# A fused attention and expert kernel on one core: keys folded before the split, token copies on ScalarE, attention copies on VectorE, later sums

## What is computed

```python
latent = (xn @ Wk + xn @ Wv) @ W_down_kv
q, k, v = heads(xn @ Wq), heads(latent @ W_up_k), heads(latent @ W_up_v)   # 16 heads of 8
scores = clip(q @ k.T / sqrt(128)) * exp(-1e-4 * abs(i - j))
attention = softmax(scores) @ v @ Wo
...
logits = xn @ Wr.T + br;  top 2 of 8 experts, softmax weights cw
z = xn + sum_e cw[e] * (gelu(xn @ W1[e].T + b1[e]) @ W2[e].T + b2[e])
experts = layer_norm(z) * ln_w + ln_b
```

## Time and profile before

| | |
|---|---|
| median of 3 runs | 271.72 us (271.06 to 271.76) |
| the profiled execution | 271.68 us, its span 269.4 us |
| PE, DVE, ACT, POOL busy | 84%, 73%, 75%, 68% of the span |
| exponentials (ACT) | 128, 1153 ns each as recorded |
| corrections (DVE) | 128, 562 ns |
| scores, outputs (PE) | 49.6 and 66.9 us busy |
| GELUs (ACT) | 156, 369 ns |
| panel copies (DVE) | 39, 996 ns |

### The profile page before, as it was taken

How to read it: one execution, slowest core, us unless ns; L and a number is a source line. 1 busy time by engine, 2 the same in 40 slices (tenths; PEclk the granted TensorE clock), 3 DMA queues, 4 the chain that set the end, 5 groups by cost and what they waited for, 6 DMA issues and landing times.

```text
span 269.4 us, 5034 instructions
## 1 busy us (share of the span) xinstructions
PE 225.9 (84%) x1673; PEld 122.7 (46%) x1673; DVE 196.0 (73%) x466; ACT 200.8 (75%) x335; POOL 182.2 (68%) x186
## 2 busy tenths in 40 slices
PE   0794557989999999998888888998788999999964
PEld 0572143879989899995122212222112231232313
DVE  2837986788988986874787876686967677667641
ACT  2557526445555565659999999999899999999950
POOL 9176708747787855594999999998899999700000
PEclk9998968999999999999999999999999999999995
DMA  6995601432217237311640169211890000000001
GB/s 202 438 439 202 175 22 39 133 134 79 67 53 179 68 74 188 78 27 49 184 112 23 29 164 217 61 29 33 207 202 2 1 21 20 0 39 2 1 39 45
DMA packets 17900, 27.46 MB, mean 102 GB/s; under 512 B 3008, under 2 KB 14944, under 8 KB 17488
## 3 DMA queue, kind: packets, MB, share of 16 engines
q1 hardware_dynamic: 15264, 22.21, 26.9%
q0 software_dynamic: 2272, 4.66, 7.4%
q10 hardware_dynamic: 336, 0.25, 0.4%
HBM read 13.01 MB, written 4.65 MB: 66 GB/s over the span
## 4 chain that ended last, share of the span: by engine, by line
PE 36%; ACT 29%; DVE 17%; issue 14%; DMA 2%; DVEq 2%; ACTq 0%
ACT shared L900 25%; PE ps L641 9%; PE ps L652 9%; PE ps L717 4%; PE ps L702 3%; DVE ps L1155 3%; PE ps L679 2%; PE ps L561 2%; DMA wvl<-w_router 2%; DVE shared L1016 2%; DVEq L1033 1%; PE ps L729 1%; DVE panels L1138 1%; DVE out_heads L1162 1%; PE ps L630 1%
## 5 line engine op out<-in xcount | busy, mean ns | idle before, releaser
L900 ACT ACTIVATE shared<-ps,rest_sb 128x1024 f32<-128x1024 f32 x128 | 130.1, 1153 | 1.7 <-DVE ps L1155 1.1
L1155 DVE TENSOR_TENSOR ps<-ps,mend_sb 128x256 f32<-128x256 f32 (+1 forms) x128 | 70.7, 562 | 29.8 <-PE ps L702 28.6
L869 ACT ACTIVATE shared<-ps,shared 128x128 f32<-128x128 f32 x156 | 44.5, 369 | 33.3 <-PE ps L641 33.3
L717 PE MATMUL ps<-shared,v_sb 128*9 128x512 f32 x512 | 66.9, 595 | 2.0 <-DVE out_heads L1162 1.2
L357 POOL DMA_INDIRECT shared<-xn_scr,source_i x39 | 46.5, 1192 | 29.4 <-PE ps L630 17.4
L702 PE MATMUL ps<-stacked 64*128 64x512 bf16 x256 | 49.6, 386 | 12.7 <-ACT shared L900 11.8
L702 PEld LDWEIGHTS ps<-stacked 64*128 64x128 bf16 x256 | 12.3, 92 | 81.4 <-ACT shared L900 73.7
L1036 DVE COPY shared<-panels 128x1156 f32 x39 | 38.8, 996 | 11.1 <-issue 10.8
L641 PE MATMUL ps<-shared 128*128 128x128 f32 x312 | 41.8, 277 | 2.4 <-DVE shared L1104 2.3
L652 PE MATMUL ps<-shared 128*128 128x128 f32 x312 | 41.5, 276 | 0.3 <-ACT shared L869 0.3
L641 PEld LDWEIGHTS ps<-shared 128*128 128x128 f32 x312 | 37.9, 192 | 3.6 <-DVE shared L1104 3.6
(11 more groups left out here) (156 smaller groups left out, 247.3 us busy)
## 6 DMA issues: line engine op xcount, KB each, us to landing
stacked<-parts SPq DMA_DIRECT2D x72, 128.0 KB, 2.6
panels<-weights SPq DMA_DIRECT2D x1, 4624.0 KB, 17.7
y_scr<-y_rows SPq DMA_DIRECT2D x19, 128.0 KB, 1.8
x_sb<-x_tiles SPq DMA_DIRECT2D x4, 256.0 KB, 4.7
xn_scr<-x_sb SPq DMA_DIRECT2D x1, 1024.0 KB, 9.0
xnT<-x_tiles SPq DMA_DIRECT2D x1, 1024.0 KB, 4.9
out<-panels SPq DMA_DIRECT2D x4, 256.0 KB, 2.0
shared<-xn_scr,source_i POOLq DMA_INDIRECT x39, 3.1
```

The lines of the kernel that those rows point to most:

```text
L717: last = nc.tensor.matmul(ps[32 * g:32 * g + VW, OUT_BANK, :], v_sb[:, b * QT + tile, h, :], probs_fast[:, duo % DUO_SLOTS, g // 2, g % 2, :],
L869: last = nc.scalar.activation(hidden[:, i % 2, c, :], ps[:, i % 2, c * P:(c + 1) * P], ACT.Gelu, bias=panel[:, i % 4, 2 * F + D + c:2 * F ...
L900: nc.scalar.activation(probs_fast[:, duo % DUO_SLOTS, couple, :, :], ps[:, score_bank(n):score_bank(n) + 2, :], ACT.Exp, scale=key_fold[:, ...
L1155: nc.vector.tensor_tensor(both, both, mend_sb[:, mends].unsqueeze(1).to_broadcast([P, 2, mends.stop - mends.start]), ALU.mult).then_inc(fa ...
```

## The change

- Keys are folded before their split: `fold_sb` has a third row, `split_step` has ten steps, five for each side, and the exponential has no scale operand.
- ACT copies the turned tokens (`keep_tokens`), in the order copy n, GELUs n-1; on PE the first widen comes ahead of the second turn. DVE loads panels two tiles ahead. DVE copies the turned attention of batches 0 to 2 (`keep_attention`) one unit after it is turned.
- The left splits of batches 0 and 1 move from tiles 10 and 20 to 21 and 27, those of batches 2 and 3 onto single units. The sums move from units 54, 64, 75, 93 to 62, 72, 86, 102. `shift_again` moves from the gathers into `finish_rest`.
- The router's bias, the top two and the copies of v are made in two parts, for tiles 0 to 5 (banks 0, 1) and 6 to 15. PE waits for both.
- After the last unit the last group's heads, its turn, division, second turn, copy (ACT), projection, addition and store go in two halves of two query tiles each, in banks of their own.

The diff, cut:

```diff
@@ -241,10 +244,13 @@
-        STATS_AT = (54, 64, 75, 93)
-        LEFT_SPLIT_AT = {2: 6, 3: 22}
+        STATS_AT = (62, 72, 86, 102)
+        LEFT_SPLIT_AT = {2: (8, 16, 24, 32, 40), 3: (48, 56, 64, 70, 78)}
...
-        PROJECT_AT = [TURN_AFTER + 2 * GROUP * group + 4 for group in PROJECT_GROUPS + (GROUPS - 1,)]
+        PROJECT_AT = [TURN_AFTER + 2 * GROUP * group + 4 for group in PROJECT_GROUPS]
+        LAST_TURN, LAST_ATTENTION, LAST_PROJECTION = (TURN_BANK, 0), (1, 2), (3, 4)
+        HALF = S // 2
...
@@ -272,8 +278,7 @@
-        LEFT_AT = (10, 20)
-        AGAIN_AT = (14, 18, 22, 26)
+        LEFT_AT = (21, 27)
...
@@ -296,46 +301,35 @@
             def split_step(b, step):
-                if step == 0:
+                side, at = divmod(step, 5)
+                kind, rows = ((RIGHT, qT_sb), (KEYS, kT_sb))[side]
+                into, ready = parts[:, b % 2, kind], parts_ready[kind]
+                done, folds = PARTS * b, 2 * (2 * b + side)
+                if at == 0:
...
-                    pool.wait_ge(qk_ready, 2 * b + 1)
-                    if b:
+                    pool.wait_ge(qk_ready, 2 * b + side + 1)
+                    if side:
+                        pool.wait_ge(parts_ready[RIGHT], done + PARTS)
+                    elif b:
...
+                    nc.gpsimd.tensor_tensor(folded[:], rows[:, b * S:(b + 1) * S], fold_sb[:, kind, :], ALU.mult).then_inc(pool_step, 1)
+                elif at == 1:
+                    pool.wait_ge(pool_step, folds + 1)
...
-                    pool.wait_ge(qk_ready, 2 * b + 2)
-                    if b >= 2:
...
+                        pool.wait_ge(rows_in[kind][b % 2], STACKED * (b // 2))
+                    nc.gpsimd.tensor_copy(into[:, 0, :], folded[:]).then_inc(ready, 1)
+                elif at == 2:
+                    pool.wait_ge(ready, done + 1)
+                    nc.gpsimd.tensor_tensor(folded[:], folded[:], into[:, 0, :], ALU.subtract).then_inc(pool_step, 1)
+                elif at == 3:
+                    pool.wait_ge(pool_step, folds + 2)
+                    nc.gpsimd.tensor_copy(into[:, 1, :], folded[:]).then_inc(ready, 1)
...
+                    pool.wait_ge(ready, done + 2)
+                    nc.gpsimd.tensor_tensor(into[:, 2, :], folded[:], into[:, 1, :], ALU.subtract).then_inc(ready, 1)
             def split(b):
-                for step in range(9):
+                for step in range(SPLIT_STEPS):
...
@@ -356,8 +349,6 @@
-                if i in AGAIN_AT:
-                    shift_again(AGAIN_AT.index(i))
             def gather(b, n):
...
@@ -410,12 +401,14 @@
             def finish_rest(b):
...
+                shift_again(b)
...
+                pool.wait_ge(xb_step, b + 2)
...
             def close(splits):
...
@@ -559,8 +561,8 @@
-                if b == B - 1:
-                    last.then_inc(vl_psum, 1)
+                    if t + 1 in ROUTED:
+                        last.then_inc(vl_psum, 1)
...
@@ -654,9 +656,12 @@
             for n in range(WORK + 1):
+                if n == 1:
+                    widen(0)
...
-                if n >= 1:
+                if n >= 2:
...
@@ -741,13 +746,32 @@
-                    if 0 <= group < GROUPS and at == 0:
+                    if 0 <= group < GROUPS - 1 and at == 0:
...
-                        pe.wait_ge(fast_done, GROUPS if b == B - 1 else PROJECT_GROUPS[b] + 1)
+                        pe.wait_ge(fast_done, PROJECT_GROUPS[b] + 1)
...
+                for half in range(2):
+                    pe.wait_ge(fast_heads, GROUPS + half)
+                    if half == 0:
+                        pe.wait_ge(fast_done, GROUPS - 1)
+                    for t in (2 * half, 2 * half + 1):
+                        last = nc.tensor.transpose(ps[:, LAST_TURN[half], t * P:(t + 1) * P], out_heads[:, t * P:(t + 1) * P], ident)
+                    last.then_inc(fast_outT, 1)
+                for half in range(2):
+                    pe.wait_ge(fast_done, GROUPS + half)
+                    for t in (2 * half, 2 * half + 1):
+                        last = nc.tensor.transpose(ps[:, LAST_ATTENTION[half], t * P:(t + 1) * P],
+                                                   attn[:, TILES - QT + t, :, :].rearrange("p h d -> p (h d)"), ident)
+                    last.then_inc(attnT_psum, 1)
+                for half in range(2):
+                    pe.wait_ge(attnT_ready, B + half)
+                    for t in (2 * half, 2 * half + 1):
+                        last = nc.tensor.matmul(ps[:, LAST_PROJECTION[half], t * D:(t + 1) * D], attnT[:, TILES - QT + t, :], wo_sb,
+                                                start=True, stop=True)
+                    last.then_inc(wo_psum, 1)
...
@@ -846,10 +870,11 @@
-            act.wait_ge(vl_psum, 1)
-            act.wait_ge(logits_ready, 1)
-            for bank in range(VL_BANKS):
-                keep_values(bank)
+            for part, (first, last) in enumerate(((0, 2), (2, VL_BANKS))):
+                act.wait_ge(vl_psum, part + 1)
+                act.wait_ge(logits_ready, part + 1)
+                for bank in range(first, last):
+                    keep_values(bank)
...
@@ -870,8 +895,18 @@
-            for i in range(WORK):
-                widened(i)
+            def keep_tokens(i):
+                act.wait_ge(xT_psum, i + 1)
+                nc.scalar.copy(x_cols[:, i % 2, :], ps[:, 4 + i % 2, 0:P]).then_inc(xT_read, 1)
+            keep_tokens(0)
+            widened(0)
+            keep_tokens(1)
+            for i in range(2, WORK):
+                keep_tokens(i)
+                widened(i - 1)
+            widened(WORK - 1)
...
@@ -883,13 +918,8 @@
-                for n in range(UNITS + 4 * GROUP):
-                    if (b := batch_at(n, PROJECT_AT, -1)) is not None:
-                        copy_attention(b)
-                    if n >= UNITS:
-                        continue
+                for n in range(UNITS):
...
-                    tile = duo % QT
...
@@ -898,7 +928,12 @@
-                                         ACT.Exp, scale=key_fold[:, tile:tile + 1]).then_inc(fast_probs, 1)
+                                         ACT.Exp).then_inc(fast_probs, 1)
+                for half in range(2):
+                    tiles = slice(2 * half, 2 * half + 2)
+                    act.wait_ge(attnT_psum, B + half)
+                    nc.scalar.copy(attnT[:, TILES - QT + tiles.start:TILES - QT + tiles.stop, :],
+                                   ps[:, LAST_ATTENTION[half], :].rearrange("p (t f) -> p t f", t=QT)[:, tiles, :]).then_inc(attnT_ready, 1)
...
+                then(nc.vector.tensor_tensor(onehot, rank, wide(ranks), ALU.is_equal))
+            for part, tiles in enumerate((slice(0, ROUTED[0]), slice(ROUTED[0], TILES))):
+                v.wait_ge(vl_psum, part + 1)
+                if part == 0:
+                    add_router_bias(slice(0, 2), VL_TILES).then_inc(logits_ready, 1)
+                else:
+                    add_router_bias(slice(VL_BANKS - 1, VL_BANKS), TILES - (VL_BANKS - 1) * VL_TILES)
+                    add_router_bias(slice(2, VL_BANKS - 1), VL_TILES).then_inc(logits_ready, 1)
+                v.wait_ge(logits_ready, part + 1)
+                top_one(tiles, logits[:, tiles, :], top[:, 0, tiles], first[:, tiles, :])
+                then(nc.vector.scalar_tensor_tensor(logits[:, tiles, :], first[:, tiles, :], -3.0e38, logits[:, tiles, :], ALU.mult, ALU.add))
+                top_one(tiles, logits[:, tiles, :], top[:, 1, tiles], second[:, tiles, :])
+                nc.vector.tensor_tensor(sel[:, tiles, :], first[:, tiles, :], second[:, tiles, :], ALU.add).then_inc(sel_ready, 1)
...
@@ -1036,6 +1080,7 @@
+            load_panel(1)
...
@@ -1097,15 +1142,10 @@
             for n in range(WORK):
-                if n < WORK:
-                    v.wait_ge(xT_psum, n + 1)
-                    if n >= 2:
-                        v.wait_ge(hT_psum, n - 1)
-                    nc.vector.tensor_copy(x_cols[:, n % 2, :], ps[:, 4 + n % 2, 0:P]).then_inc(xT_read, 1)
-                if n + 1 < WORK:
-                    load_panel(n + 1)
...
+                if n + 2 < WORK:
+                    load_panel(n + 2)
...
@@ -1170,6 +1210,11 @@
+                def keep_attention(b):
+                    v.wait_ge(attnT_psum, b + 1)
+                    nc.vector.tensor_copy(attnT[:, b * QT:(b + 1) * QT, :],
+                                          ps[:, TURN_BANK, :].rearrange("p (t f) -> p t f", t=QT)).then_inc(attnT_ready, 1)
...
-                    if 0 <= group < GROUPS and at == 0:
+                    if 0 <= group < GROUPS - 1 and at == 0:
...
+                    if (b := batch_at(n, PROJECT_AT, 1)) is not None:
+                        keep_attention(b)
...
+                v.wait_ge(fast_used, QT * GROUPS)
+                v.wait_ge(fast_outT, GROUPS - 1)
+                for half in range(2):
+                    queries = slice(half * HALF, (half + 1) * HALF)
```

(19 more changed lines are left out.)

110 lines of the change are left out of this document (42 added, 68 removed).

## The result

The changed kernel takes 270.62 us in the median of 19 runs (267.86 to 271.84), the kernel before 271.76 (270.39 to 272.68). The ratio is 0.9957, 95% interval 0.9936 to 0.9977: 1.1 us faster where I had forecast 10.2, and outside my range. The profiled execution took 270.61 us with a span of 268.8.

A forecast was written before the change was run, and what follows sets the result against it. PE bounds the expert stage; ACT only just bounds the attention, a PE-DVE chain 0.03 us behind. From 271.68: -5.9 - 0.4 - 1.2 - 0.8 - 0.5 + 0 - 1.4 = -10.2, so 261.5 us; range 257.5 to 267.

The forecast's parts named there:

- The exponential without its operand: Attention: 0.905 us a unit instead of 0.997, ordinary groups of 8 units 7.49 instead of 7.98; twelve groups give -5.9.
- (a): Attention: the unscaled exponential costs more, 0.96 us a unit, an ordinary group 7.77; total 265 us; chance 0.15.
- (b): Attention: the operand's read is hidden, the exponential stays at 0.997 us; total 267.5 us; chance 0.10.
- (c): Attention: DVE's queue has more room than walked, the new wait doesn't appear; total 258.5 us; chance 0.12.
- (d): Expert stage: ACT's in-order queue binds and lengthens every tile, 2.2 us if its loop takes 4.4; total 273; chance 0.05.
- (e): POOL and prologue losses (collisions, a late rest) eat nearly everything: no change; chance 0.03.
- the prologue: Router's top two partly in DVE's idle time, narrower instructions, against POOL collisions: 0, from -0.8 to +0.8 us.
- the start of the expert stage: Copy 1 waits for GELU 0, first narrow 1.1 us later; panel 7 ahead of the verdict, 0.8 more: +1.9.
- Projection groups: Three attention groups whose turned-attention copy moves from ACT to DVE: 0.4 us less each, -1.2 in all.
- Expert tiles: Tiles stay at 1.89 us; long panel copies go because POOL's ln_b additions leave the stage: three times 0.8, -2.4.
- Tail: After the last unit, heads to store in halves: -1.4 us, between -0.7 and -2.2.
- splits and sums: Attention: moving VectorE's left splits onto single units and the sums later gives -0.8 us, bounds -2.5 and +1.5.

The follow-up runs named there:

- again_early: Changed kernel with GpSimd's four ln_b additions back in the expert stage, at gathers 14, 18, 22 and 26: 269.89 us.
- tokens01: Changed kernel with the token copies of expert tiles 0 and 1 back on VectorE and the first two widens in the old order: 265.98 us.
- verdict_late: tokens01 with TensorE's verdict turn moved from tile 6 to 8 and VectorE's decision from 8 to 10: 263.60 us.
- router_whole: Changed kernel with the router's top two taken in one piece for all 16 tiles: 271.36 us.
- pool_short: Changed kernel with GpSimd's twenty split steps of batches 2 and 3 cut to 16 of 512 columns: 267.10 us.
- after_scaled: Changed kernel with the exponential reading a scale per partition again, a column of ones: 273.15 us.
- combined2: verdict_late with left splits of batches 2 and 3 in expert tiles 22-26 and 28-32, and batch 1's sums in unit 70 instead of 72: 258.14 us.
- before_unscaled: Kernel before the change with only the exponential's scale operand taken away: 268.64 us.
- old_places: Changed kernel with VectorE's left split steps and sums in the units of the kernel before: 272.71 us.

## Why the prediction was wrong

**Right.** The exponential without its operand: 0.905 apart in units 4 to 7, 7.50 for an ordinary group (forecast 7.49), the gap ahead of unit 3 and a correction at its end, so the new wait through PE and the heads copy is where the walk put it. For this rate the Trainium skill's figures (ScalarE: Activation LUTs, What ACT_TABLE_LOAD costs) had given 0.946; the trace decides for the constant taken from the copies. Rivals (a), (b), (c) and (d) fall; (e), to which I gave 0.03, came nearest: collisions ate about half of what was lost, though in the attention and not in the prologue, and the other half went at the start of the expert stage, which (e) doesn't name; ACT's order never made a running tile longer than 1.90. Projection groups: 8.95 to 8.97 for the forecast 8.83, about 0.3 less than before each. Expert tiles: the 2.4 came in full, though for another reason than I gave (again_early). GpSimd's late rest: nobody waited, though it was ready at 215.5, not 208.8. Tail: -1.6 from the last exponential's end where I had -1.4, since the clock held: both halves of the last product took 1.16 together, not 2.08.

```profile
264.06 1.16 PE L772 MATMUL ps<-rest_sb,kT_sb 128*128 128x128 f32 x8
...
265.33 1.51 SPq L500 DMA_DIRECT2D out<-panels  x2
```

**Wrong, first: the start of the expert stage, +1.9 in the sum, +5.7 measured** (first exponential +4.4, less +1.1 of the prologue, plus the 2.4 that the later tiles gained). I saw copy 1 behind GELU 0 and a panel ahead of the verdict, and priced both at what the waiting engine loses in the wait. I left out that copy 0 stands behind ScalarE's squares (0.61 at 45.06), and that TensorE's clock falls in such waits: its products then take up to 2.08 for 1.06. The verdict's wait itself I had at 0.8 more, and it was 1.95 more (2.28 for 0.33). With the copies back (tokens01) and the verdict two tiles later (verdict_late) 3.0 and 3.5 of it go, in profiles. The clock's part varies: in router_whole, whose expert stage is the same, it stayed at full level behind the verdict's wait, and from the sources' copy to the first exponential it took 87.4, 2.0 less than in after.

**Wrong, second and as large: splits and sums, -0.8 with an upper bound of +1.5.** The twelve ordinary groups had to give 6.7 with this term; they gave 2.0, so the term was +3.9. My bound had ten steps and four sums each meeting one instruction of GpSimd for 0.2 (on top of -0.8 that makes +2.0, not the +1.5 in the text). The ten steps took 13.0 us where undisturbed ones take 5.8, that is 0.7 more each. The prologue's row of 1.07 for 0.29, 0.8 more in one meeting, stood in front of me, and I had quoted the Trainium skill (SBUF - State Buffer, Who interferes with whom) for the prologue alone. By its rule each of the six steps (of the ten) that have two inputs in SBUF could wait for the whole of an instruction of 1.2: the trace agrees, and goes beyond it, since a step waited for two in a row (2.79). The casts wait as well (1.55 and 1.60 in after, 1.23 in pool_short), which the same section allows for copies and casts in a faster mode. Why it cost time here is what after_scaled shows. From unit 7 to 55 the first six steps took 5.2 longer than undisturbed ones in after, and the groups 3.3 longer than in combined2, which has no steps there; in after_scaled the steps took 3.5 longer and the groups only 0.8. At 0.997 a unit most of such a delay falls into VectorE's slack, at 0.905 the chain through VectorE is the bound and most of it is paid. **The slack that would have hidden the collisions was what the faster exponential spent.** In my own walk that slack was 0.03 us once a group, and I still priced the steps as if it were there. Nor were the collisions all there before: the ten steps took 6.7 us in before, 9.0 in before_unscaled and 8.4 in old_places, and 13.0 in the single units to which I moved them. So a part of this term came with the move that should have saved something.

**Wrong, third and small: the prologue, 0 with bounds of 0.8, +1.1 in the profiled pair.** Of this some 0.4 is the added fold less the cut, the rest scatter.

Made up again: +4.9 at the first exponential, +4.7 in the ordinary groups, +0.2 in the first and the projection groups, -0.7 at the tail and around the span are the 9.1 between 261.5 and 270.6.

## What to carry to other kernels

When an engine that bounds a stage is made faster, first list what runs in its shadow, price each item by the worst meeting that the trace holds anywhere (here 0.8, in the prologue), and take that as paid in full for an upper bound; here 6.3 us of gain became 3.6 in the kernel before and 2.0 to 2.5 in the one after. Put VectorE's work on SBUF where GpSimd only issues gathers, not where it computes on SBUF, and when work is moved, look at what GpSimd does in the new place. Price a wait of TensorE with the products behind it at the low clock, and look at the first tiles of a stage by themselves when an in-order engine gets a new task.
